# One AdaLN-FFN kernel, a new instruction order on all engines and a new share of the elementwise work

## What is computed

```python
# _bi_wkv: r = x, k = v = fside, decay from w and cond
a = a * decay + ekv_t ; b = b * decay + ek_t      # forward and reverse scan
num = nf + nb - ekv + euk * vf
den = df + db - ek + euk
out = sigmoid(r) * (num / max(den, 1e-8)) * (0.8 + 0.2 * tf)
# layer 0: gate = argmax(softmax(xf @ Wg.T)); y = 4 * prob_sel * Bw[gate] @ (A[gate] @ xf)
# layer 1: h = gelu(x @ w1_q.T + b1); out = h @ w2_q.T + b2, w_q ternary by 0.7 * mean(|w|)
```

## Time and profile before

| | us |
|---|---|
| median of the three runs | 126.23 |
| profiled execution, its time | 126.34 |
| its span (first to last instruction) | 124.5 |
| VectorE busy | 108.2 |
| TensorE matmul busy | 101.1 |
| ScalarE busy | 83.0 |
| GpSimd busy | 51.7 |

### The profile page before, as it was taken

How to read it: one execution, slowest core, us unless ns; L and a number is a source line. 1 busy time by engine, 2 the same in 40 slices (tenths; PEclk the granted TensorE clock), 3 DMA queues, 4 the chain that set the end, 5 groups by cost and what they waited for, 6 DMA issues and landing times.

```text
span 124.5 us, 2082 instructions
## 1 busy us (share of the span) xinstructions
PE 101.1 (81%) x654; PEld 93.7 (75%) x654; DVE 108.2 (87%) x218; ACT 83.0 (67%) x148; POOL 51.7 (42%) x61
## 2 busy tenths in 40 slices
PE   5596791099987999699725999967989799989991
PEld 5485790099976889599524899956979799989990
DVE  1389999999999999999999997999999999994731
ACT  4186989940676934469248549878099996997441
POOL 3077484817071149095703528409440390000530
PEclk9999689756999599999985599999999999999999
DMA  3899990000000000000000000000000002020004
GB/s 91 278 311 304 309 382 13 0 8 0 0 0 0 0 0 3 5 3 0 0 0 3 0 0 0 5 0 0 0 0 5 0 0 84 0 87 5 0 3 168
DMA packets 7271, 6.44 MB, mean 52 GB/s; under 512 B 2370, under 2 KB 7004, under 8 KB 7260
## 3 DMA queue, kind: packets, MB, share of 16 engines
q1 hardware_dynamic: 7244, 6.31, 16.3%
q10 hardware_dynamic: 16, 0.00, 0.0%
HBM read 5.26 MB, written 1.05 MB: 51 GB/s over the span
## 4 chain that ended last, share of the span: by engine, by line
DVE 58%; PE 17%; issue 17%; DMA 2%; DVEq 1%; ACT 1%; ACTq 0%
DVE run L708 14%; DVE nd L726 11%; PE bank L1134 6%; DVE own L695 4%; PE bank L1054 4%; DVE hm L776 4%; DVE mask L768 3%; PE bank L1101 3%; DVE nd L738 3%; DVE run L716 2%; DMA vec_rows<-in_L_cond_u_dram 2%; DVE nd L250 2%; DVE h_lo L262 2%; DVE nd L236 2%; DVE nd L223 2%
## 5 line engine op out<-in xcount | busy, mean ns | idle before, releaser
L708 DVE TENSOR_TENSOR_SCAN run<-bank,kv 128x256 f32<-128x256 f32 x32 | 20.1, 669 | 0.4
L726 DVE TENSOR_TENSOR_SCAN nd<-bank,run 128x256 f32<-128x256 f32 x32 | 20.1, 673 | 0.2
L1054 PE MATMUL bank<-hm,BT 128*128 128x256 f32 x64 | 16.9, 423 | 1.5 <-DVE hm L776 1.5
L1038 PE MATMUL bank<-nd,AT 128*128 128x256 f32 x64 | 17.7, 431 | 0.0
L1101 PE MATMUL bank<-xin_hi,w1T 128*128 128x256 f32 x64 | 15.8, 287 | 1.7 <-ACT h L536 1.2
L1054 PEld LDWEIGHTS bank<-hm,BT 128*128 128x128 f32 x64 | 13.6, 217 | 4.2 <-DVE hm L776 1.9
L262 POOL TENSOR_TENSOR h_lo<-h,h_hi 128x512 fp32r<-128x512 f32 x6 | 8.1, 1348 | 20.4 <-DVE h_hi L270 14.0
L1134 PE MATMUL bank<-w2T,h_hi 128*128 128x256 f32 x64 | 15.9, 287 | 0.5 <-DVE h_lo L262 0.5
L1038 PEld LDWEIGHTS bank<-nd,AT 128*128 128x128 f32 x64 | 15.8, 330 | 0.4
L1134 PE MATMUL bank<-w2T,h_lo 128*128 128x256 f32 x64 | 15.3, 278 | 0.0
L1101 PE MATMUL bank<-xin_lo,w1T 128*128 128x256 f32 x64 | 15.2, 279 | 0.0
(11 more groups left out here) (131 smaller groups left out, 236.5 us busy)
## 6 DMA issues: line engine op xcount, KB each, us to landing
w_nat<-in_L_ffn_w_dram SPq DMA_DIRECT2D x2, 1024.0 KB, 8.1
F_nat<-in_fside_BxSxS_dram SPq DMA_DIRECT2D x4, 256.0 KB, 4.1
x_nat<-in_x_dram SPq DMA_DIRECT2D x4, 256.0 KB, 5.0
out_dram<-outb SPq DMA_DIRECT2D x3, 256.0 KB, 2.1
A_nat<-in_L_ffn_A_dram SPq DMA_DIRECT2D x1, 512.0 KB, 5.7
B_nat<-in_L_ffn_Bw_dram SPq DMA_DIRECT2D x2, 256.0 KB, 6.7
out_dram<-outb SPq DMA_DIRECT2D x2, 128.0 KB, 1.7
vec_rows<-in_L_cond_w_dram ACTq DMA_DIRECT2D x2, 1.0 KB
```

The costliest lines, as they stand in the source:

```text
L708: dve.tensor_tensor_scan(run[:, r, c, q], decay_ps[:, l, c, b:b + 1].broadcast_to([P, T]), kv[:, b, c, q], 0.0, ALU.mult, ALU.add).then_in ...
L726: dve.tensor_tensor_scan(nd[:, r, c, q, ::-1], decay_ps[:, l, c, b:b + 1].broadcast_to([P, T]), run[:, r, c, q, ::-1], 0.0, ALU.mult, ALU. ...
L1038: mm = pe.matmul(bank[H_BANK + k][:, (m % 2) * T:(m % 2 + 1) * T], AT[:, c, m::NM], nd[:, r, c, NUM, :], start=(c == 0), stop=(c == NC - 1))
L1054: mm = pe.matmul(bank[y_bank[b % 2]][:, o * T:(o + 1) * T], BT[:, m, o * P:(o + 1) * P], hm[:, b % 2, m], start=False, stop=(o == NC - 1 a ...
```

## The change

All instructions stay. Their order is new in the lists of GpSimd, ScalarE, VectorE and TensorE, and some elementwise steps are issued on another engine. Counted in instructions of 512 elements with two inputs (L210 to L262): GpSimd 37 before and 35 after, less one copy-like clip in both; VectorE 31 and 33. `result(2)` and `last_result(0)` go from ScalarE to VectorE. ScalarE has ten table loads in place of twelve. The SP list is the same. The indentation is left off below.

```diff
--- before.py
+++ after.py
@@ -369,45 +369,43 @@
                        ALU.add).then_inc(factors_ready, 1)
 
 gains()
-times_values(pool, 0)
-clip_keys(pool, 1)
+factors()
 times_values(pool, 1)
-factors()
 own_values(pool, 0, 0)
+add_den(pool, 0, 1)
+add_den(pool, 0, 0)
+clip_keys(pool, 2)
 own_values(pool, 0, 1)
-add_den(pool, 0, 0)
+times_sigmoid(pool, 0)
 add_num(pool, 0, 1)
-add_num(pool, 0, 0)
-num_times_rec(pool, 0, 0)
+times_values(pool, 2)
 den_times_rec(pool, 0, 1)
 num_times_rec(pool, 0, 1)
-own_values(pool, 0, 3)
-add_den(pool, 0, 2)
+own_values(pool, 0, 2)
 den_times_rec(pool, 0, 2)
+own_values(pool, 1, 0)
+add_den(pool, 0, 3)
 add_num(pool, 0, 2)
-num_times_rec(pool, 0, 2)
+add_den(pool, 1, 0)
 times_sigmoid(pool, 2)
-own_values(pool, 1, 0)
-times_values(pool, 3)
-add_den(pool, 1, 0)
+den_times_rec(pool, 0, 3)
+den_times_rec(pool, 1, 0)
 add_num(pool, 1, 0)
-den_times_rec(pool, 1, 0)
 num_times_rec(pool, 1, 0)
-den_times_rec(pool, 0, 3)
-num_times_rec(pool, 0, 3)
-xin_low(pool, 0)
 add_den(pool, 1, 1)
+add_num(pool, 0, 3)
+den_times_rec(pool, 1, 1)
 own_values(pool, 1, 1)
-den_times_rec(pool, 1, 1)
 add_num(pool, 1, 1)
-h_low(pool, 0, 0)
-h_low(pool, 0, 3)
-xin_low(pool, 1)
+num_times_rec(pool, 1, 1)
+h_low(pool, 0, 1)
+own_values(pool, 1, 2)
+own_values(pool, 1, 3)
 h_low(pool, 1, 1)
-h_low(pool, 1, 2)
-own_values(pool, 1, 3)
-h_low(pool, 3, 1)
-h_low(pool, 3, 2)
+den_times_rec(pool, 1, 2)
+xin_low(pool, 2)
+h_low(pool, 2, 0)
+h_low(pool, 3, 3)
 
 @block.scalar
 def _(act):
@@ -542,111 +540,107 @@
 scaled_values(0)
 u_exps()
 key_exp(1)
-scaled_values(1)
-scaled_values(2)
 key_exp(2)
-evacuate_Wg()
 act.preload_act_table_set("sigmoid_and_others")
 sigmoid(0)
+scaled_values(1)
+evacuate_Wg()
 sigmoid(1)
-scaled_values(3)
 sigmoid(2)
 sigmoid(3)
-evacuate_A(0)
-evacuate_A(1)
-evacuate_B(0)
-evacuate_B(1)
+scaled_values(2)
 act.preload_act_table_set("natural_log_exp_and_others")
 key_exp(3)
-abs_sum(0)
+log_den(0, 1)
+evacuate_A(0)
 log_den(0, 0)
 reciprocal(0, 0)
+evacuate_B(0)
+evacuate_A(1)
+evacuate_B(1)
+abs_sum(0)
 abs_sum(1)
-log_den(0, 1)
+scaled_values(3)
 reciprocal(0, 1)
 sign_below(0)
+sign_above(0)
 gate_exp(0)
-sign_above(0)
+sign_above(1)
+log_den(0, 2)
+evacuate_wT(0)
+reciprocal(0, 2)
 copy_mask(0)
-sign_above(1)
+evacuate_wT(1)
+evacuate_wT(2)
+log_den(0, 3)
+evacuate_wT(3)
 gate_exp(1)
-log_den(0, 2)
-reciprocal(0, 2)
-evacuate_wT(0)
+sign_below(1)
+reciprocal(0, 3)
+log_den(1, 0)
+reciprocal(1, 0)
+keep_x1(0)
+copy_mask(1)
+evacuate_wT(4)
+gate_exp(2)
+evacuate_wT(5)
 act.preload_act_table_set("gelu_and_others")
 tanh(0)
-keep_x1(0)
-evacuate_wT(1)
-copy_mask(1)
-evacuate_wT(2)
-sign_below(1)
-evacuate_wT(3)
+keep_x1(1)
+tanh(1)
+evacuate_wT(6)
 act.preload_act_table_set("natural_log_exp_and_others")
-gate_exp(2)
-log_den(1, 0)
-evacuate_wT(4)
-reciprocal(1, 0)
-log_den(0, 3)
-reciprocal(0, 3)
+log_den(1, 1)
+evacuate_wT(7)
 copy_mask(2)
-evacuate_wT(5)
-keep_x1(1)
-evacuate_wT(6)
-act.preload_act_table_set("gelu_and_others")
-tanh(1)
 xin_high(act, 0)
-keep_x1(2)
-tanh(2)
-evacuate_wT(7)
-act.preload_act_table_set("natural_log_exp_and_others")
-gate_exp(3)
-log_den(1, 1)
 reciprocal(1, 1)
 act.preload_act_table_set("gelu_and_others")
 gelus(0, 0)
+act.preload_act_table_set("natural_log_exp_and_others")
+gate_exp(3)
+act.preload_act_table_set("gelu_and_others")
+gelus(0, 1)
 h_high(act, 0, 0)
-copy_mask(3)
-gelus(0, 1)
+xin_high(act, 1)
 gelus(0, 2)
-h_high(act, 0, 2)
 h_high(act, 0, 1)
 gelus(0, 3)
-h_high(act, 0, 3)
-xin_high(act, 1)
-keep_x1(3)
-tanh(3)
+copy_mask(3)
+keep_x1(2)
+gelus(1, 0)
+tanh(2)
+h_high(act, 1, 0)
+gelus(1, 1)
+h_high(act, 1, 1)
 act.preload_act_table_set("natural_log_exp_and_others")
 log_den(1, 2)
 reciprocal(1, 2)
+h_high(act, 0, 3)
+log_den(1, 3)
+reciprocal(1, 3)
 act.preload_act_table_set("gelu_and_others")
-gelus(1, 0)
-gelus(1, 1)
-h_high(act, 1, 1)
+tanh(3)
 gelus(1, 2)
+xin_high(act, 2)
+keep_x1(3)
 h_high(act, 1, 2)
 gelus(1, 3)
 h_high(act, 1, 3)
+gelus(2, 0)
 result(act, 0)
-act.preload_act_table_set("natural_log_exp_and_others")
-log_den(1, 3)
-reciprocal(1, 3)
-act.preload_act_table_set("gelu_and_others")
-gelus(2, 0)
-h_high(act, 2, 0)
 gelus(2, 1)
-result(act, 1)
-h_high(act, 2, 1)
-xin_high(act, 3)
 gelus(2, 2)
 gelus(2, 3)
-h_high(act, 2, 3)
+h_high(act, 2, 1)
+result(act, 1)
 gelus(3, 0)
+h_high(act, 2, 2)
 h_high(act, 3, 0)
 gelus(3, 1)
 gelus(3, 2)
+h_high(act, 3, 1)
 gelus(3, 3)
-result(act, 2)
-last_result(act, 0)
 
 @block.vector
 def _(dve):
@@ -794,134 +788,138 @@
 decays()
 clip_keys(dve, 0)
 forward(0, 0, DEN)
+times_values(dve, 0)
+clip_keys(dve, 1)
 inverse_gains()
+forward(0, 1, DEN)
 seed(0, 0, DEN)
+own_keys(0, 1)
+seed(0, 1, DEN)
+own_keys(0, 0)
+backward(0, 1, DEN)
+forward(0, 0, NUM)
 backward(0, 0, DEN)
-forward(0, 0, NUM)
-forward(0, 1, DEN)
-own_keys(0, 0)
-own_keys(0, 1)
+seed(0, 0, NUM)
 forward(0, 1, NUM)
+backward(0, 0, NUM)
+forward(0, 2, DEN)
+own_keys(0, 2)
+add_num(dve, 0, 0)
+den_times_rec(dve, 0, 0)
+num_times_rec(dve, 0, 0)
 seed(0, 1, NUM)
-seed(0, 0, NUM)
+seed(0, 2, DEN)
 backward(0, 1, NUM)
-seed(0, 1, DEN)
+own_keys(0, 3)
+ratio(0, 0)
+clip_keys(dve, 3)
+backward(0, 2, DEN)
 forward(1, 0, NUM)
-backward(0, 0, NUM)
+thresholds()
+gate(0)
+forward(0, 3, DEN)
+forward(0, 2, NUM)
+forward(1, 0, DEN)
+gate_index(0)
+times_sigmoid(dve, 1)
+seed(0, 2, NUM)
+seed(1, 0, DEN)
+add_den(dve, 0, 2)
+own_keys(1, 0)
+expert_mask(0)
+times_values(dve, 3)
 seed(1, 0, NUM)
-backward(0, 1, DEN)
-clip_keys(dve, 2)
-own_keys(0, 2)
-add_den(dve, 0, 1)
-times_values(dve, 2)
-forward(0, 2, DEN)
-seed(0, 2, DEN)
-den_times_rec(dve, 0, 0)
-times_sigmoid(dve, 0)
-ratio(0, 0)
-thresholds()
-backward(0, 2, DEN)
-gate(0)
-gate_index(0)
-own_keys(0, 3)
-times_sigmoid(dve, 1)
-expert_mask(0)
+seed(0, 3, DEN)
 ratio(0, 1)
-own_values(dve, 0, 2)
+backward(0, 3, DEN)
 select_expert(0, 1)
 select_expert(0, 0)
+backward(0, 2, NUM)
 gate(1)
+backward(1, 0, DEN)
 gate_index(1)
-forward(0, 2, NUM)
+num_times_rec(dve, 0, 2)
 expert_mask(1)
-seed(0, 2, NUM)
-backward(0, 2, NUM)
+forward(1, 1, DEN)
 forward(1, 1, NUM)
-seed(1, 1, NUM)
-forward(1, 0, DEN)
-seed(1, 0, DEN)
-backward(1, 0, DEN)
-clip_keys(dve, 3)
+own_keys(1, 1)
+seed(1, 1, DEN)
 ratio(0, 2)
-own_keys(1, 0)
+backward(1, 0, NUM)
 select_expert(1, 0)
 select_expert(1, 1)
 gate(2)
+forward(0, 3, NUM)
+backward(1, 1, DEN)
+seed(0, 3, NUM)
+own_values(dve, 0, 3)
+backward(0, 3, NUM)
+ratio(1, 0)
+forward(1, 3, DEN)
 gate_index(2)
-backward(1, 0, NUM)
-forward(0, 3, DEN)
-seed(0, 3, DEN)
-backward(0, 3, DEN)
+num_times_rec(dve, 0, 3)
 expert_mask(2)
-own_keys(1, 1)
-add_den(dve, 0, 3)
-forward(0, 3, NUM)
-seed(0, 3, NUM)
-backward(0, 3, NUM)
+ffn_input(0)
+times_sigmoid(dve, 3)
+seed(1, 1, NUM)
+ratio(0, 3)
+xin_low(dve, 0)
 select_expert(2, 1)
+backward(1, 1, NUM)
+gate(3)
+forward(1, 2, DEN)
 select_expert(2, 0)
-ratio(1, 0)
-ffn_input(0)
-add_num(dve, 0, 3)
-forward(1, 1, DEN)
-seed(1, 1, DEN)
-times_sigmoid(dve, 3)
-ratio(0, 3)
-backward(1, 1, DEN)
-gate(3)
+forward(1, 2, NUM)
+ratio(1, 1)
 gate_index(3)
-forward(1, 3, DEN)
+ffn_input(1)
+expert_mask(3)
+seed(1, 2, DEN)
+xin_low(dve, 1)
+own_keys(1, 3)
 seed(1, 3, DEN)
-forward(1, 2, NUM)
-expert_mask(3)
+seed(1, 2, NUM)
+h_low(dve, 0, 0)
 own_keys(1, 2)
-seed(1, 2, NUM)
-backward(1, 1, NUM)
-own_values(dve, 1, 2)
+backward(1, 3, DEN)
 select_expert(3, 1)
 select_expert(3, 0)
-forward(1, 2, DEN)
-num_times_rec(dve, 1, 1)
-h_low(dve, 0, 1)
-ratio(1, 1)
-ffn_input(1)
-seed(1, 2, DEN)
 backward(1, 2, DEN)
+add_den(dve, 1, 2)
+forward(1, 3, NUM)
+add_den(dve, 1, 3)
+h_low(dve, 1, 0)
 backward(1, 2, NUM)
-add_den(dve, 1, 2)
+h_high(dve, 0, 2)
+add_num(dve, 1, 2)
 h_low(dve, 0, 2)
-add_num(dve, 1, 2)
-own_keys(1, 3)
 num_times_rec(dve, 1, 2)
-den_times_rec(dve, 1, 2)
+seed(1, 3, NUM)
 ratio(1, 2)
-h_high(dve, 1, 0)
 ffn_input(2)
-h_low(dve, 1, 0)
-forward(1, 3, NUM)
-seed(1, 3, NUM)
-backward(1, 3, DEN)
-xin_high(dve, 2)
-xin_low(dve, 2)
-add_den(dve, 1, 3)
+h_low(dve, 0, 3)
 backward(1, 3, NUM)
 add_num(dve, 1, 3)
+h_low(dve, 1, 2)
+num_times_rec(dve, 1, 3)
+den_times_rec(dve, 1, 3)
+ratio(1, 3)
+ffn_input(3)
+xin_high(dve, 3)
 h_low(dve, 1, 3)
-den_times_rec(dve, 1, 3)
-num_times_rec(dve, 1, 3)
-ratio(1, 3)
-h_low(dve, 2, 0)
-ffn_input(3)
+h_high(dve, 2, 0)
+xin_low(dve, 3)
+h_high(dve, 2, 3)
+h_low(dve, 2, 2)
 h_low(dve, 2, 1)
-xin_low(dve, 3)
-h_high(dve, 2, 2)
-h_low(dve, 2, 2)
 h_low(dve, 2, 3)
 h_low(dve, 3, 0)
-h_high(dve, 3, 1)
+h_low(dve, 3, 1)
 h_high(dve, 3, 2)
+h_low(dve, 3, 2)
 h_high(dve, 3, 3)
-h_low(dve, 3, 3)
+result(dve, 2)
+last_result(dve, 0)
 last_result(dve, 1)
 
 @block.tensor
@@ -1149,100 +1147,100 @@
 transpose_x(1)
 transpose_x(2)
 transpose_Wg()
+transpose_x(3)
+transpose_B(0)
+transpose_B(1)
 transpose_F(3)
-transpose_x(3)
 transpose_A(0)
 transpose_A(1)
-transpose_B(0)
-transpose_B(1)
-place_residual(0)
-place_residual(1)
-weight_totals()
 keep_warm(fwd_done[NUM][0], 2, 6)
 keep_warm(bwd_done[NUM][0], 2, 8)
```

(83 more changed lines are left out.)

## The result

The changed kernel takes 120.12 us (median of four executions, 119.61 to 120.87) beside 126.27 us for the kernel before on the same chip. The ratio is 0.9501, with a 95% interval of 0.9463 to 0.9539, so it is 5.0% faster. I had said 125.4 us, with a range down to 122.9. The direction was right, with a chance of 0.47 given to "faster", and the size was far too small.

The account below looks back on a forecast made before the run. VectorE was taken to bound the kernel up to the third mask (71.6 us), then TensorE to 120.9; plus 2.64 us of tail and 1.84 outside the span this gave 125.4 us, range 122.9 to 128.3.

Parts of the forecast that it names:

- What bounds the kernel: Kernel before: VectorE until the last ffn_input, then TensorE almost without a gap to 121.86 us.
- Part 1, VectorE up to the third mask: VectorE's list through expert_mask(2): start 7.2, work 51.4 and waits 13.0 make the mask ready at 71.6 us.
- the 13.0 us for waits beside GpSimd: VectorE before the third mask: waits when it and GpSimd shut each other out, taken between 12.2 and 14.3 us.
- ten meetings found by hand: VectorE instructions expected to stand beside GpSimd ones before the third mask, 0.95 to 1.35 us each, together 11.6.
- the walk's 12.2: Laying the five engine lists side by side gave VectorE 12.2 us of waits, hand-overs included, before the third mask.
- Part 2, TensorE's run: TensorE from transpose_mask(2) at 71.7 us: 47.9 us of work plus 1.3 us, ending at 120.9.
- the 1.3 us for clock and feeding: Added to TensorE's run behind the third mask for slow clock and late inputs, from bounds of 0 and 2.8 us.
- The two feeding waits: TensorE: ffn_out(0,3) waits 0.65 us for h_low(0,3), hidden(2,0) 0.45 us for GpSimd's xin_low(2).
- Part 3, the rest: Behind ffn_input(3): moved result copies taken as 0 us, two fewer ScalarE table loads 0 on the path.
- (b): Rival, fewer losses: the walk's 12.2 us hold and TensorE keeps its clock, 123.3 us; chance 0.20.
- (a): Rival: more VectorE-GpSimd meetings before the third mask, 1.27 us each, up to 128.3 us; chance 0.28.
- (c): Rival: mask early enough, but ScalarE's list or place_output(0) holds TensorE another 0.8 us, 126.2 us; chance 0.16.

Follow-up runs that it names:

- e8: Kernel before, with 24 idle TensorE transposes behind transpose_weights(5) and 5 ahead of expert_out(2): 126.82 us, ratio 1.0007.
- e3: Changed kernel with 26 idle TensorE transposes behind transpose_mask(1) and 6 ahead of expert_out(1): 119.26 us, ratio 0.9450.
- e11: Changed kernel with result(2) and last_result(0) back on ScalarE: 120.47 us, ratio 0.9535.
- e14: Changed kernel with the edits of e12 and e11 together: 118.23 us, ratio 0.9340.
- e10: Changed kernel with the two ScalarE table loads of the kernel before put back: 120.74 us, ratio 0.9543.
- e5: Changed kernel without any edit, timed again: 121.19 us, ratio 0.9547.
- e12: Changed kernel with the idle transposes of e3, and gate(2) moved behind forward(0, 3, NUM) on VectorE: 118.03 us, ratio 0.9332.

## Why the prediction was wrong, point by point

**What bounds the kernel** held for the kernel before: e8 shows its TensorE can be made 1.7 us faster at `expert_out(2)` for nothing.

**Part 1, VectorE up to the third mask: the term that failed most.** The failed step is the 13.0 us for waits beside GpSimd. The trace has 59.9 us from the first clip at 6.45 to the mask at 66.35; less the 51.4 us of work that leaves 8.5 us for waits. Of the ten meetings found by hand nine took place. They cost 0.8 to 1.1 us each, about 8.9 together, where I gave 11.6 for ten, so the work with its hand-overs was about 51.0 us and that term was right. The tenth, `own_values(0,3)`, went the other way: VectorE was there first, and GpSimd waited (1.63 us for its 1.27). Then I moved the walk's 12.2 up to 13.0, by the sentence "a walk misses meetings and doesn't invent them". It did invent one, and the correction made an error of 3.7 us one of 4.5. The rate of the kernel before (0.62 us per GpSimd instruction) is a property of its order, and a new order is what was being predicted; in it the same count gives 0.37. Another 0.73 us is the start, where VectorE waited less for its first inputs; the profiles of the changed kernel and its variants begin their first clip between 6.33 and 7.05 us, the two of the kernel before at 7.18 and 7.38, so some of this scatters and whether the rest belongs to the order stays open.

**Part 2, TensorE's run.** From the transposes of the third mask to its end TensorE took 47.4 us (68.23 to 115.64) against my 47.9. Nothing was added to it: the 1.3 us for clock and feeding were not paid there. The two feeding waits that I saw in the walk did not come: TensorE is busy in full in every stage from 64 to 112 us. The clock was paid, 3.0 us of it, but ahead of the mask, where TensorE already was the chain. I had a hint in my own text: TensorE was to be idle for some 2 to 3 us ahead of the third mask, at full clock, and I did not ask what becomes of that if VectorE is earlier and `expert_out(1)` slower. The mask was ready 5.3 us before my 71.6, and TensorE took it up 1.9 us late. That this second error made the miss smaller was luck: with the clock kept (e3) the time is 119.3.

**Part 3, the rest.** The tail behind TensorE's end is 3.26 us, not 2.64. The moved copies are not its cause: with them back on ScalarE it is 3.6 us in the profiles of e11 and e14. What the cause is stays open. The two table loads are worth less than the times can tell, though not quite nothing (0.70 us of wait in e10). In the trace after, the next instruction starts 1.30 us behind the start of a load (59.67 and 60.97 us):

```profile
59.08 0.57 ACT L515 ACTIVATE w2T<-bank 128x512 fp32r<-128x512 f32 x1
59.67 1.28 ACT L587 ACT_TABLE_LOAD   x1
60.97 0.60 ACT L520 ACTIVATE sig<-bank 128x512 f32<-128x512 f32 x1
```

The 2.66 us for a switch, drain included, of the Trainium skill (ScalarE: Activation LUTs, section "What ACT_TABLE_LOAD costs") are thus not seen here either, neither ahead of the load nor behind it; the load by itself took 1.28 us.

**The sum.** From 125.4: TensorE takes up the third mask 3.47 us earlier (68.23 for 71.7), 0.49 less work, 1.3 not paid, 0.62 more tail and 0.13 more outside the span. That gives 120.9, the profiled execution.

**The rivals.** (b), fewer losses, was the right direction at 123.3 and stopped short, because it took the walk itself as the best case. (a) had the wrong sign, and (c), the gain used up, didn't come about. The range failed for the same reason: its low end left no room for a walk that is too slow.

**The signs.** The third mask was done at 66.35, not between 70.8 and 72.5, and the mean mask instruction was 576 ns, not near 807, with two of the eight beside GpSimd work as foretold. VectorE stood idle for 1.50 us before 70 us, for ScalarE's `xin_high(0)`, which I had named as a sign of being wrong; it lies behind the third mask and cost nothing there. TensorE was full, and the clock from 64 us on was granted in full: no clock loss behind the mask.

## What to carry to other kernels

When all engines have fixed lists, find for each engine the last point at which it still waits, and ask of each term in which engine's chain it lies there: 1.7 us of slow clock were worth nothing in one order, and of 3.0 us in the other some 0.9 (medians) to 1.7 (profiled executions) reached the end. A gap of some 3 us on TensorE right ahead of a long call on the path is worth filling with idle products; it took off 0.9 us and most of the scatter. A call moved on one list has to be moved with the calls of other engines that wait for it, or the experiment measures the queueing.

## What was not expected of the hardware

Where the low clock falls varies between executions of one kernel: `expert_out(1)` took from 5.10 to 6.69 us in ten profiles with the gap ahead of it, and 3.69 with the gap filled. The executions lie 1.3 us apart in the changed kernel, 1.0 in e5, 0.17 in e3 and 0.25 in e12, so I put most of that scatter down to it. For the executions without a profile that is not shown. The two shortest of the changed kernel even have the lowest mean granted clock, 0.899, beside 0.914 and 0.923; a low stretch that begins earlier, under idle time, would give that. Between VectorE and GpSimd the one that came first went first in these rows, and the other was stretched. In the changed kernel VectorE's product began 0.17 us ahead of GpSimd's:

```profile
60.77 0.68 DVE L216 TENSOR_TENSOR own<-own,vs 128x512 f32<-128x512 f32 x1
...
60.94 1.63 POOL L223 TENSOR_TENSOR nd<-nd,own 128x512 f32<-128x512 f32 x1 [2.50 <-DVE nd L720]
```

The 1.2 us that I had laid on VectorE here cost it nothing (its next instruction starts 0.60 us later, the price of the work alone), and GpSimd 0.36.
